# Two fused transformer layers on one core: three layer-norm means move from VectorE to GpSimd, one scale step is dropped, and the four engines' orders are written anew

## The reference, cut to what matters

```
layer 0:  h = norm(x)*(1+ca)+sa                       # norm a0
          x = x + ga * (norm(h + y@Wout + bout)*g+b)  # y: linear attention with two decay rates
                                                      # (scans over 256 tokens); norm z0
          h = norm(x)*(1+cb)+sb                       # norm f0
          x = x + gb * ffn(h)
layer 1:  h = norm(x)*(1+ca)+sa                       # norm a1
          x = x + ga * rwkv(h)   # time mix (inner norm b1, recurrence) and channel mix (norm c1)
          h = norm(x)*(1+cb)+sb                       # norm f1
          x = x + gb * ffn(h)
ffn(x):   silu(q(x)@q(Wg)) * (q(x)@q(Wu)) -> q(.) @ q(Wd)
q(x):     per block of 16: scale = max(max|x| / 6, 1e-12); x/scale is rounded to the grid
          0, .5, 1, 1.5, 2, 3, 4, 6 with its sign, and multiplied by scale
```

## Time and profile before

| what | value |
|---|---|
| median of 3 runs | 1400.71 us |
| the profiled execution | 1395.93 us |
| its span | 1394.0 us |
| busy in the span: PE, DVE, ACT, POOL | 88%, 80%, 76%, 16% |
| mean granted TensorE clock | 0.957 of full speed |

### The profile page before, as it was taken

The page is one execution under the profiler, slowest core; times in us unless marked ns, Lnnn a source line. Parts: engine busy times, 40 slices in busy tenths (PEclk is TensorE's granted clock), DMA queues, the critical chain, the costliest instruction groups (busy, mean ns, idle before and its releaser), DMA issues.

```text
span 1394.0 us, 18809 instructions
## 1 busy us (share of the span) xinstructions
PE 1228.5 (88%) x5710; PEld 732.2 (53%) x5710; DVE 1121.0 (80%) x1619; ACT 1062.6 (76%) x2849; POOL 222.7 (16%) x286
## 2 busy tenths in 40 slices
PE   5677888989899999989898999989898999979787
PEld 2234364655656564646556564746455555647453
DVE  5848587988989798979889897979798897965424
ACT  5163868889797979798797979797897979786653
POOL 1000202121211103021212111030212112110100
PEclk9888999999999999999999999999999999989899
DMA  4000000000000000000000000000000000000000
GB/s 133 0 0 8 1 1 8 1 16 1 16 1 16 1 15 2 1 16 1 16 1 16 1 16 1 9 8 1 16 1 16 1 16 1 9 1 8 0 8 8
DMA packets 21488, 13.67 MB, mean 10 GB/s; under 512 B 1552, under 2 KB 20624, under 8 KB 21392
## 3 DMA queue, kind: packets, MB, share of 16 engines
q1 hardware_dynamic: 12944, 8.29, 2.0%
q10 hardware_dynamic: 8448, 4.20, 1.0%
HBM read 8.28 MB, written 4.19 MB: 9 GB/s over the span
## 4 chain that ended last, share of the span: by engine, by line
PE 67%; ACT 12%; DVE 11%; issue 6%; POOL 3%; SPq 0%; DMA 0%; ACTq 0%; DVEq 0%; POOLq 0%
PE ps L1105 10%; PE ps L1218 6%; PE ps L1317 4%; PE ps L923 4%; PE ps L1310 4%; PE ps L1184 3%; PE ps L1017 3%; PE ps L1256 3%; PE ps L1013 3%; PE ps L903 3%; PE ps L1257 3%; ACT hq L502 2%; PE ps L977 2%; PE ps L937 2%; POOL rstd_of_a L411 2%
## 5 line engine op out<-in xcount | busy, mean ns | idle before, releaser
L1105 PE MATMUL ps<-wguT,hqcol 128*128 128x352 f32 x512 | 168.2, 470 | 20.4 <-ACT hqcol L676 12.5
L1569 DVE TENSOR_TENSOR_SCAN state<-beta,outer 128x512 f32<-128x512 f32 x128 | 149.2, 1206 | 0.0
L1105 PEld LDWEIGHTS ps<-wguT,hqcol 128*128 128x128 f32 x512 | 93.1, 191 | 78.2 <-issue 24.6
L418 POOL TENSOR_TENSOR var_of_f<-squares_f,eps_sum 128x4 f32<-128x4 f32 x32 | 12.1, 378 | 656.3 <-ACT hq L502 656.3
L1419 DVE SCALAR_TENSOR_TENSOR hid<-hidcol,hid 128x1408 f32<-128x1408 f32 (+1 forms) x68 | 106.2, 1566 | 6.0 <-ACT hidcol L693 5.9
L1218 PE MATMUL ps<-hidcol,wdT 128*128 128x256 f32 (+1 forms) x384 | 92.5, 384 | 0.4 <-ACT hidcol L702 0.4
L1641 DVE TENSOR_TENSOR hid<-th,ps 128x352 f32<-128x352 f32 x128 | 63.3, 512 | 25.2 <-ACT th L684 16.2
L977 PE MATMUL ps<-state,const 128*32 128x512 f32 x256 | 70.9, 831 | 8.8 <-DVE state L1595 8.4
L1595 DVE TENSOR_TENSOR state<-state,qshare 128x1024 f32<-128x1024 f32 x64 | 76.8, 1221 | 2.2
L903 PE MATMUL ps<-const,hq 128*128 128x128 f32 x128 | 34.8, 335 | 48.7 <-ACT hq L492 47.4
L700 ACT ACTIVATE hidcol<-ps 128x512 f32<-128x512 f32 x64 | 38.1, 595 | 51.6 <-PE ps L1184 51.6
(11 more groups left out here) (236 smaller groups left out, 3291.4 us busy)
## 6 DMA issues: line engine op xcount, KB each, us to landing
xa<-in_x SPq DMA_DIRECT2D x16, 256.0 KB, 2.8
out<-xb ACTq DMA_DIRECT2D x16, 256.0 KB, 2.2
const<-in_const SPq DMA_DIRECT2D x1, 848.0 KB, 6.5
state<-in_wmod SPq DMA_DIRECT2D x1, 768.0 KB, 4.5
outer<-in_wqk SPq DMA_DIRECT2D x1, 256.0 KB, 4.5
ex<-in_w_gate_up SPq DMA_DIRECT2D x2, 128.0 KB, 2.6
fw_key<-in_fw_key SPq DMA_DIRECT2D x1, 256.0 KB, 3.0
fw_val<-in_fw_val SPq DMA_DIRECT2D x1, 256.0 KB, 3.8
```

The lines of the kernel that those rows point to most:

```text
L1105: t_.matmul(bank(f"f{l}_{'gu'[g]}{t}")[:, 0:I_FF], hqcol[l][:, t * P:(t + 1) * P], wguT[:, l, g, :], start=True, stop=True).then_inc(s_gu[ ...
L1569: return v.tensor_tensor_scan(state[:, m, c, :], beta[:, m, :], src, 0.0, ALU.mult, ALU.add)
```

## The change

`scale_blocks` has no `back` any more (its own instruction, L1408): the rows are scaled with a negative factor, so that the scale itself serves for putting back. The three means are taken off DVE's list and stand in POOL's, each right ahead of the power of its norm. `xa` and `xb` hold three pairs and not two. All `body` lists start at another place of the same cycle (a step of pair n-3 at the end of a turn is what pair n-2 was at its start), and within the cycle some steps change places. `BANK` and the waits of `freed` are made anew for that order; the numbers of `run_idle` products stay.

```diff
-        xa = sb("xa", [P, 2 * NT, H])      # xb likewise
+        xa = sb("xa", [P, 3 * NT, H])
...
-    load_x: before_last(sp, s_x2mm, i)
+    load_x: if i >= 3: sp.wait_ge(s_x2mm, i - 2)
...
             def scale_blocks(part, src, dst, scales, at, nb):
-                    v.tensor_scalar(back, top, -put_back, -SCALE_MIN, ALU.mult, ALU.min)
-                    return v.tensor_scalar(scale, top, 1 / 6.0, floor, ALU.mult, ALU.max)
+                    return v.tensor_scalar(scale, top, 1 / 6.0, SCALE_MIN, ALU.mult, ALU.max)
-                return v.scalar_tensor_tensor(dst, src, TIE_DOWN, spread(inv, nb), ALU.mult, ALU.mult)
+                return v.scalar_tensor_tensor(dst, src, -TIE_DOWN, spread(inv, nb), ALU.mult, ALU.mult)
...
-                return v.tensor_tensor(dst, dst, spread(scales[:, 3, at:at + nb], nb), ALU.mult)
+                return v.tensor_tensor(dst, dst, spread(scales[:, 1, at:at + nb], nb), ALU.mult)
```

The means, on POOL (mean_a1 and mean_f0 have the same form), and POOL's list:

```diff
+            def mean_f1(j):
+                pool.wait_ge(s_x3, j + 1)
+                before(pool, s_norm["f1"], j, NT)
+                g.tensor_scalar(of_two(negm["f1"], j), sums["f1"][:, :], -1.0 / H, None, ALU.mult).then_inc(s_mean["f1"], 1)
...
             def body(n):
-                power_b1 n-3, power_z0 n-2, power_f0 n-2, power_c1 n-3, power_f1 n-3, power_a1 n-2, power_a0 n
+                mean_f1 n-3, power_f1 n-3, mean_a1 n-2, power_a1 n-2, power_a0 n, power_b1 n-2, power_z0 n-1,
+                mean_f0 n-1, power_f0 n-1, power_c1 n-2
```

The places in the orders of which the prediction speaks, in short form (steps in the order of the list, pair numbers left out, l = 0 or 1 for the layer):

```diff
 ACT, around the end of the FFN of layer 0
-  b6g(1) b6g(1) c9 c9 b5(0,0) b6c(1) a3t store b5(0,1) c8 a1b b6g(0) b6g(0) b1v(1) b6c(0) c1v c1n.. a1n c1 c1 a1 c2s a5y a1
+  b6g(1) a1b b6g(1) a3t c9 c9 b6c(1) b5(0,0) c8 store b5(0,1) b1v(1) b6g(0) b6g(0) b6c(0) c1v c1n.. c1 c1 a1n c2s a1 a5y a1
 ACT, after a6s
-  c2 a3 b2(1) a6n a3s a7 a7 b3(1,0) c4 c4 load c4e c4 c4 a8 c4e b1v(0) a2 load b3 c3 b3 b1n(0) b3 b1c b1c
+  c2 b2(1) a6n a3 a7 a7 b3(1,0) a3s c4 c4 load c4e c4 a8 c4 b1v(0) c4e a2 load b3 b3 b1n(0) b3 c3 b1c b1c
 ACT, later
-  c5s b2(0) b4(1) b3(0,0) b3(0,1) c5m b3(0,2) c5n ..
+  c5s b2(0) b4(1) c5m b3(0,0) b3(0,1) c5n c5x a3s b3(0,2) ..
 DVE
-  a4(0,0) a5(0) a4(0,1) a5(1) mean_f1 a5(2) a4(1,0) mean_a1 a5q a5q a4m a4m a1s
+  a4(0,0) a5(0) a5(1) a4(0,1) a5(2) a4(1,0) a5q a5q a4m a4m a1s
-  b3(1,0) c4b a3b c4s mean_f0 c4s c4v c4n c4p a2p(0) a3(0) .. b1m(3) b4(1,2) b1q b1q b1q .. b4(0,0) a2p(1)
+  a3b b3(1,0) c4b c4s c4s c4n a2p(0) c4v a3(0) .. b1m(3) b4(1,2) a2p(1) b1q b1q b1q .. b4(0,0)
 PE
-  b1T_1 a4(0,0) a4(0,1) b1R_1 a4(1,0) c1 a1 c1r a4(1,1) a6
+  b1T_1 a4(0,0) b1R_1 a4(0,1) c1 a4(1,0) c1r a1 a4(1,1) a6
-  a3b(1) a2(0) c3(2) a3(0) b3_1 b3_1 b3_1 b1T_0 a2(1) b1R_0 a3(1) c5 c7x b2(0) b3_0 b3_0 b3_0 c5n b3_0 c6r
+  a2(0) b3_1 c3(2) a3(0) b3_1 b3_1 b1T_0 a2(1) b1R_0 a3(1) a3b(1) c5 c7x b2(0) b3_0 b3_0 c5n b3_0 b3_0 c6r
```

More of the change, by code:

```diff
@@ L382, in _ @@
             turns(sp, body)
-            for p in range(2):
-                sp.wait_ge(s_out[p], 8 * PAIRS)
+            for p in range(3):
+                sp.wait_ge(s_out[p], 16 * len(range(p, PAIRS, 3)))
         @block.gpsimd
@@ L448, in body @@
             def body(n):
[L449 to L452, removed]
+                do(mean_f1, n - 3)
                 do(power_f1, n - 3)
+                do(mean_a1, n - 2)
                 do(power_a1, n - 2)
                 do(power_a0, n)
+                do(power_b1, n - 2)
+                do(power_z0, n - 1)
+                do(mean_f0, n - 1)
+                do(power_f0, n - 1)
+                do(power_c1, n - 2)
             turns(pool, body)
@@ L500, in spread_squares @@
                 for t in range(NT):
-                    at = (i % 2) * NT + t
-                    ins = s.activation(spare[:, t, :], rows[:, at, :], ACT.Square, bias=negm[ln][:, at:at + 1],
+                    ins = s.activation(spare[:, t, :], of_pair(rows, i)[:, t, :], ACT.Square, bias=of_two(negm[ln], i)[:, t:t + 1],
                                        accum_out=squares[ln][:, t:t + 1])
@@ L843, in body @@
                 do(c1n, n - 2)
-                do(a1n, n)
                 do(c1, n - 2, 0)
                 do(c1, n - 2, 1)
+                do(a1n, n)
+                do(c2s, n - 2)
                 do(a1, n, 0)
-                do(c2s, n - 2)
                 do(a5y, n - 1)
@@ L1382, in body @@
                 do(b3_1, n - 3, 0)
+                do(a8, n - 1)
                 do(c3, n - 2, 1)
-                do(a8, n - 1)
+                do(a2, n, 0)
+                do(b3_1, n - 3, 1)
+                do(c3, n - 2, 2)
+                do(a3, n, 0)
+                do(b3_1, n - 3, 2)
+                do(b3_1, n - 3, 3)
+                do(b1T_0, n - 1)
+                do(a2, n, 1)
+                do(b1R_0, n - 1)
+                do(a3, n, 1)
+                do(a3b, n, 1)
+                do(c5, n - 2)
+                do(c7x, n - 2)
+                do(layer(b2, 0), n - 1)
+                do(b3_0, n - 1, 0)
+                do(b3_0, n - 1, 1)
+                do(c5n, n - 2)
+                do(b3_0, n - 1, 2)
+                do(b3_0, n - 1, 3)
+                do(c6r, n - 2)
             turns(pe, body)
@@ L1399, in spread, with scale_blocks @@
                 return t.unsqueeze(2).to_broadcast([P, nb, BLK])
-            def scale_blocks(part, src, dst, scales, at, nb, put_back, floor):
-                top, scale, inv, back = (scales[:, k, at:at + nb] for k in range(4))
+            def scale_blocks(part, src, dst, scales, at, nb):
+                top, scale, inv = (scales[:, k, at:at + nb] for k in range(3))
                 if part == 0:
```

582 lines of the change are left out of this document (281 added, 301 removed), and 10 rows, old and new, of the table BANK.

## The result

The changed kernel takes 1415.34 us (median of 4 runs, 1410.52 to 1418.10), the kernel before 1400.74 beside it (4 runs, 1400.48 to 1401.14): ratio 1.010, 95% interval 1.0073 to 1.0128. Predicted were 1383.5, range 1364 to 1402. The profiled execution took 1418.1 us with a span of 1416.2, against 1394.0 of before.

A forecast was written before the change was run, and what follows sets the result against it. PE, busy 88%, was taken to bound the kernel, except in the boundary, where the chain leaves it. Boundary gains of 20.2 us less 2.9 at the end took 1395.93 to 1378.6; 4.78 for the median gave 1383.5, range 1364 to 1402.

The forecast's parts named there:

- The clock: TensorE's clock as an error bar: half-speed products for a few us at either end, worth 3 us each way.
- Boundary, 1.85 us: Stretch from f1's norm to `a6`: the mean off DVE and reordered steps start `a6` 1.85 us earlier each turn.
- Body, a loss of 0.4: Rest of the turn, PE nearly dense: moved ACT and DVE steps make PE wait, losing 0.4 us a turn.
- new waits of PE on freed banks: Listed sign of being wrong: PE waiting for reassigned PSUM banks; could not be priced, taken as nothing.
- Mean of f1 held, 0.15: `mean_f1` on POOL among DVE's scans: 0.15 us a turn added, a third of a half-microsecond hold.
- rival C: DVE holds POOL's instructions, making the kernel slower: 1419 us, near 1408 if half the turns are hit; chance 0.14.
- Scale step, 0.2 to 0.4 us of DVE a turn: Dropped scale instruction: some 0.4 us a turn leave DVE, 0.2 ahead of `wy`; counted within the body's sum.
- Table loads, 2.9: End of kernel: four table loads now behind the last store lengthen the span by 2.9 us.
- Means, as a whole: Means moved to POOL: without `mean_a1` ahead, `a5q` starts earlier, so DVE's boundary chain comes 0.8 us earlier.
- Rival B: The mean is hidden anyway: POOL's powers of a1 and a0 keep PE's time; 1400.5 us, chance 0.10.

The follow-up runs named there:

- e4: Kernel before plus three unread PE products ahead of the f1 transposes in every turn: 1396.42 us, ratio 0.9977 to the kernel before.
- e3: Changed kernel plus three unread PE products ahead of the f1 transposes in every turn: 1398.31 us, ratio 0.9994 to the kernel before.
- f2: Kernel before with only the three means moved to POOL, plus three unread products ahead of the f1 transposes every turn: 1399.74 us, ratio 0.9982.
- h2: As e3, with PE's last `a4` ahead of `a1`'s transposes and ACT's `a5y` ahead of `a1`: 1400.08 us, ratio 0.9975 to the kernel before.
- h5: As e3, with DVE's `a2p(1)` back behind `b1q`: 1398.36 us, ratio 0.9964 to the kernel before.
- f5: As f3, with `f1_u0` in PSUM bank 6 instead of 0: 1393.74 us, ratio 0.9943 to the kernel before.
- f1: As e3, with the three means back on DVE: 1413.54 us, ratio 1.0075 to the kernel before.
- f3: As e3, without the four table loads of the last turn: 1395.91 us, ratio 0.9957 to the kernel before.
- g3: Repeat of e4, the kernel before with three unread products ahead of the f1 transposes every turn: 1398.13 us, ratio 0.9993.
- g1: Changed kernel with three unread products every turn ahead of layer 1's FFN transposes, where PE is nearly dense: 1443.63 us, ratio 1.0307 to the kernel before.

## Why the prediction was wrong

One turn in three pieces, from the traces (gate to `a6`; `a6` to the first FFN product that waits for `hqcol`; from there to the next gate):

| kernel | gate to `a6` | to the FFN | to the gate | turn |
|---|---|---|---|---|
| e4, before with its clock | 16.22 | 31.83 | 28.80 | 76.85 |
| e3, after with its clock | 15.39 | 32.32 | 28.91 | 76.62 |
| after, the turn shown | 16.60 | 32.33 | 28.91 | 77.84 |

1. **The clock: the step that failed first.** I wrote "Products at half speed for a few us at either end are worth 3 us each way", and took them for a matter of start and end. The clock falls in ten of eleven boundaries of both kernels. It costs the kernel after 1.21 us in the turn of the table, all of it in the boundary, and 15 to 17 us in all (e3, by ratios or by medians), and the kernel before 0.09 us a turn (76.94 against 76.85 in e4). The earlier trace rows had the sign: 0.98 for a full turn is not 1. The earlier trace rows showed the idle 2.77 us, and the trace the products of 1.92 beside those of 0.98. What I missed is that they were mostly free only because PE waited for DVE between them (0.80 us, e4), and that the reordered lists ended this.
2. **Boundary, 1.85 us: it was 0.83 with the clock.** Two terms. "The products that `a5q` needs start at 674.37, the first four of eight are there by 675.0": where no mean stands ahead of it, `a5q` starts when all eight have ended (3.15 us after the gate in after, 3.14 in f2), though the program makes its first half wait for the first four alone, and why stays open. So DVE came 0.36 and not 0.8 us earlier. And "PE's last `a4` no longer waits behind `c1r` ... but only for the last `a4m`" overlooked `a1`'s transposes, which wait for ACT's `a1n`, now behind `c1`: the last `a4` starts 0.6 us after `a4m` ended (838.97 against 837.16 + 1.23 in e3). h2 shows that this wait can't be had back for nothing.
3. **Body, a loss of 0.4: it was 0.60** (0.49 and 0.11). The size held. Of the 0.49, `a2p(1)` carries 0.24 (32.32 to 32.08 in h5), near the 0.3 that I gave it; but taking it back does not shorten the turn, so something else takes over, and which of the moved steps that is stays open. The new wait for a bank, "new waits of PE on freed banks, which I could not price", does not carry the loss (f5).
4. **Mean of f1 held, 0.15:** the hold is there, 0.54 us against 0.23 for the mean of a1, and the addition and the power behind it are held as well, but in the boundary shown ACT is busy until the mean is done, so it cost nothing. The rival C had named this mechanism; its price was no part of the 32 us, and even so the means on POOL are worth 0.95 us a turn in this order (f1). The Trainium skill, "GPSIMD Engine Reference" (1. Specifications), has GpSimd contend with VectorE instructions that have two SBUF inputs; these rows agree, scans included. The result lies within the 1408 to 1419 us that I gave C, but not by its mechanism.
5. **Scale step, 0.2 to 0.4 us of DVE a turn:** worth 0.12 of the turn. **Table loads, 2.9:** 3.2 by the traces, 2.4 by f3. The Trainium skill, "ScalarE: Activation LUTs" (What ACT_TABLE_LOAD costs), adds a drain to each switch; between these loads the trace shows none.
6. **Means, as a whole.** I argued the 0.8 us from the mean of a1 and DVE's wait alone, as if the order did not matter. The order decides: nothing in the old one, 0.95 in the new one, which without the means on POOL is slower than the old one (77.57 against 76.85). By the pieces of f1's turn those 0.95 come from the mean of f1 ahead of the gate, not from the mean of a1.

By the sum: predicted 1.3 us a turn, measured 0.23 with the clock held, which over 14 turns is 15 us; the clock is 17 us by the medians; together the 32 us between 1383.5 and 1415.3, to within the 2 us by which the two measures of the clock differ. The start, 4.4 us later in the profiled execution, can't be split further: in e3 `a0` of pair 4 starts at 297.51, but one and the same kernel has it at 299.47 in e4 and at 296.05 in g3. Rival B, "the mean is hidden anyway", describes the old order (f2) and, by its number, the new one with its clock (e3, 1398.3).

## What to carry to other kernels

Before shortening a chain, list what runs slow or late beside it without cost, and ask for each whether the new order puts it on the chain; here that was TensorE at its lower clock behind an idle gap. A full turn's granted clock under 1 is a term of every turn, and unread products in the gap ahead of it are a cheap test, and here a cheap cure. And measure a moved step in both orders: the same move gave 0 and 15 us.

## What the runs showed of the hardware

- 2.7 us of idle PE were followed by products at half clock, one or two groups of four `a4` records at up to 1.92 us for 1.05, in most turns, but not in all: the turn of the kernel after that escaped (76.64 us) had all its `a4` at 1.05. Three unread products that fill the gap kept the clock at 1.00 over the whole turn (e3, e4); three at a busy place did not (1.92 us in g1).
- GpSimd's multiplication of 128x4 took 0.23 us beside `a5q`, 0.54 among scans and 1.06 in f2 (858.86); its power 1.01 at best and up to 1.91 in the boundary.
- Four table loads behind one another took 1.29 us each, beside a store of 256 KB that was landing in 2.2 us, and moved the end by 3.2 us.
